# x_b of two chunks by DMA instead of by selection, and another order of the opening

## The reference

```python
Ws = [W0, W1, W2]                       # W0 40x40x100, W1 and W2 40x100x100
curr = base = inputs                    # 512 x 40 x 16
for Wk, bk in zip(Ws, bs):
    z = jnp.einsum('bid,bjd->bdij', base, curr)
    curr = jnp.einsum('bdij,ijh->bhd', z, Wk) + bk[None, :, None]
    logit.append(curr)
pooled = jnp.sum(jnp.concatenate(logit, axis=1), axis=-1)
out = pooled @ lin_w + lin_b            # 512 x 1
```

## Time and profile before

| | us |
|---|---|
| median of 3 runs | 181.58 |
| lowest and highest run | 181.56, 182.77 |
| profiled execution | 181.67 |
| its span | 179.9 |

### The profile page before, as it was taken

How to read it: one execution, slowest core, us unless ns; L and a number is a source line. 1 busy time by engine, 2 the same in 40 slices (tenths; PEclk the granted TensorE clock), 3 DMA queues, 4 the chain that set the end, 5 groups by cost and what they waited for, 6 DMA issues and landing times.

```text
span 179.9 us, 2520 instructions
## 1 busy us (share of the span) xinstructions
PE 175.2 (97%) x798; PEld 118.7 (66%) x798; DVE 152.1 (85%) x138; ACT 73.7 (41%) x79; POOL 13.0 (7%) x20
## 2 busy tenths in 40 slices
PE   6999989999999999999999999999999999999994
PEld 2374557777777777777777777677777777777760
DVE  0696896399999999999999999999999999993022
ACT  2535750064642464236432644264426442530021
POOL 3631624000000000000000000000000000000000
PEclk9999999999999999999999999999999999999999
DMA  5998834999978587857795778477957740000000
GB/s 188 381 413 317 231 87 120 417 416 410 281 229 296 163 236 227 319 141 230 229 327 143 233 226 315 149 231 225 283 182 233 226 133 0 0 4 0 0 0 0
DMA packets 12038, 37.06 MB, mean 206 GB/s; under 512 B 2481, under 2 KB 3325, under 8 KB 12030
## 3 DMA queue, kind: packets, MB, share of 16 engines
q1 hardware_dynamic: 11066, 36.36, 61.4%
q10 hardware_dynamic: 868, 0.32, 0.8%
q0 software_dynamic: 96, 0.27, 0.6%
HBM read 35.88 MB, written 1.07 MB: 205 GB/s over the span
## 4 chain that ended last, share of the span: by engine, by line
PE 95%; POOL 1%; issue 1%; DVE 1%; ACT 1%; ACTq 0%; DVEq 0%; POOLq 0%
PE c_ps L456 42%; PE q_ps L456 42%; PE q_ps L509 4%; PE q_ps L544 2%; PE c_ps L500 1%; PE q_ps L500 1%; POOL wc_low L422 1%; PE q_ps L520 1%; PE q_ps L465 1%; PE q_ps L547 1%; PE c_ps L594 1%; PE c_ps L597 0%; DVE acc L326 0%; DVE w_post L270 0%; ACT out_sb L404 0%
## 5 line engine op out<-in xcount | busy, mean ns | idle before, releaser
L337 ACT ACTIVATE z_high<-xb_z 126x1024 fp32r<-126x1024 f32 x56 | 59.2, 1061 | 79.3 <-DVE xb_z L249 79.1
L256 DVE TENSOR_TENSOR z_low<-xb_z,z_high 126x1024 fp32r<-126x1024 f32 x56 | 68.9, 1233 | 0.9 <-ACT z_high L337 0.8
L249 DVE TENSOR_TENSOR xb_z<-x_a,xb_z 126x1024 f32<-126x1024 f32 x50 | 61.0, 1220 | 9.4 <-DMA xb_z<-xw 9.3
L456 PE MATMUL c_ps<-z_high,wc_high 126*101 126x512 f32 x112 | 35.4, 396 | 0.7 <-POOL wc_low L422 0.7
L456 PE MATMUL c_ps<-z_low,wc_high 126*101 126x512 f32 x112 | 35.0, 394 | 0.0
L456 PE MATMUL c_ps<-z_high,wc_low 126*101 126x512 f32 x112 | 35.0, 394 | 0.0
L456 PE MATMUL q_ps<-z_high,wq_high 126*101 126x512 f32 x108 | 33.9, 395 | 0.0
L456 PE MATMUL q_ps<-z_high,wq_low 126*101 126x512 f32 x108 | 33.8, 394 | 0.0
L456 PE MATMUL q_ps<-z_low,wq_high 126*101 126x512 f32 x108 | 33.7, 393 | 0.0
L456 PEld LDWEIGHTS c_ps<-z_high,wc_high 126*101 126x101 f32 x112 | 18.3, 165 | 9.1 <-POOL wc_low L422 1.2
L456 PEld LDWEIGHTS c_ps<-z_high,wc_low 126*101 126x101 f32 x112 | 18.5, 165 | 7.5
(11 more groups left out here) (56 smaller groups left out, 60.6 us busy)
## 6 DMA issues: line engine op xcount, KB each, us to landing
xb_z<-xw SPq DMA_DIRECT2D x50, 512.0 KB, 4.3
x_a<-xa SPq DMA_DIRECT2D x8, 512.0 KB, 4.9
w_post<-w1x SPq DMA_DIRECT2D x4, 512.0 KB, 8.6
w_d<-w2h SPq DMA_DIRECT2D x4, 404.0 KB, 6.1
pair_sb<-w_pairs SPq DMA_DIRECT2D x1, 404.0 KB, 11.6
d_dram<-w_d SPq DMA_DIRECT2D x2, 189.4 KB, 2.8
d_dram<-w_d SPq DMA_DIRECT2D x4, 94.7 KB, 2.6
pair_sb<-d_dram ACTq DMA_DIRECT2D x3, 82.9 KB
```

The source lines that it names most:

```text
L249: nc.vector.tensor_tensor(xb_z[0:K, c, :], x_a[0:K, u % 2, :], x_b, ALU.mult).then_inc(z_done, 1)
L256: nc.vector.tensor_tensor(z_low[0:K, m % SLOTS, :], xb_z[0:K, c, :], z_high[0:K, m % SLOTS, :].bitcast(fp32), ALU.subtract).then_inc(low_d ...
L337: nc.scalar.activation(z_high[0:K, m % SLOTS, :], xb_z[0:K, m % C, :], ACT.Copy).then_inc(high_done, 1)
L456: last = nc.tensor.matmul(ps[0:J, h * B:(h + 1) * B], w[0:K, c * J:(c + 1) * J], z[0:K, slot, h * B:(h + 1) * B], start=(c == 0 and k == 0 ...
```

## The change

- x_b of chunks 5 and 6 of unit 0 is loaded by SP behind W0's last piece; TensorE makes the selections 1 to 4 only. Form 5 and form 6 wait for these loads.
- Warm-up: 12 matmuls instead of 20, then one fp32 matmul on acc. V piece 0 goes ahead of selections 1 and 2.
- SP: the four loads of W2 go ahead of W0's second piece. One 25 KB store of D goes from POOL to SP.
- VectorE: split 2 goes ahead of form 3, split 3 ahead of form 5, and the copy of d group 2 is done by VectorE behind form 4, with a semaphore of its own.
- ScalarE: select_r is rounded before chunk 0, round_high(0, 2) goes ahead of the copy of the v rows, cast_w0(1) behind the copies of v and the constant, round_high(0, 3) ahead of copy_d(3).
- POOL: low_w0(0) goes ahead of sum_w0(1).

```diff
--- before.py
+++ after.py
@@ -18,6 +18,7 @@
 BODY = 2 * C
 PRODUCT_AT = 16
 C1_AT = 2 * C - 1
+SELECTED = 4
 
 VP = 4
 VG = 5
@@ -41,7 +42,7 @@
 RIGHT = P + T - 1 + C - 1 - F
 DW = LEFT + F + RIGHT
 DB = 48
-DS_SP, DS_POOL = 7, 3
+DS_SP, DS_POOL = 8, 2
 WC_CUTS = (0, 1, 3, C)
 WQ_CUTS = (0, 2, C)
 PREP_CUTS = (0, 2, 4, C)
@@ -51,7 +52,7 @@
 
 LOW_AT = 64
 SW = 128 + C - 1
-WARM = 20
+WARM = 12
 E_AT = 0
 Z_AT = E_AT + DR
 ZW = QT + VG
@@ -135,6 +136,7 @@
         const_done = sem("const_done")
         const_copied, select_rounded = sem("const_copied"), sem("select_rounded")
         dgroup_done, dgroup_copied = sem("dgroup_done"), sem("dgroup_copied")
+        dgroup_copied_dve = sem("dgroup_copied_dve")
         wc_sums, wc_highs, wc_ready = sem("wc_sums"), sem("wc_highs"), sem("wc_ready")
         wq_sums, wq_highs, wq_ready = sem("wq_sums"), sem("wq_highs"), sem("wq_ready")
         last_sums, last_highs, last_ready = sem("last_sums"), sem("last_highs"), sem("last_ready")
@@ -193,21 +195,24 @@
             load_xb(0, 0)
             load_w0(0)
             sp.dma_start(small_sb[:, :], small).then_inc(small_loaded, 16)
-            load_w0(1)
             for i in range(VP):
                 load_w2(i)
+            load_w0(1)
             for i in W1_ORDER:
                 load_w1(i)
             load_w0(2)
+            for c in range(SELECTED + 1, C):
+                load_xb(0, c)
             sp.wait_ge(dgroup_copied, 1)
             store_d(sp, 0, LEFT + 4 * GI, 4 * GI, LOWER - 4 * GI, (8, 8 + DB))
             sp.wait_ge(dgroup_copied, 3)
             store_d(sp, 0, LEFT, 0, 2 * GI, (0, DB))
             store_d(sp, 1, LEFT + UPPER_AT[0], 0, 2 * GI, (DR - DB, DR))
-            sp.wait_ge(dgroup_copied, 4)
+            sp.wait_ge(dgroup_copied_dve, 1)
             store_d(sp, 0, LEFT + 2 * GI, 2 * GI, GI, (0, DB))
             store_d(sp, 1, LEFT + UPPER_AT[2], 2 * GI, GI, (DR - DB, DR))
-            sp.wait_ge(dgroup_copied, 5)
+            store_d(sp, 1, 0, 3 * GI - (LEFT - 2 * GI), LEFT - 2 * GI, (0, 32))
+            sp.wait_ge(dgroup_copied, 4)
             store_d(sp, 0, LEFT + 3 * GI, 3 * GI, GI, (4, 4 + DB))
             store_d(sp, 1, LEFT + UPPER_AT[3], 3 * GI, GI, (10, 10 + DB))
             sp.wait_ge(equals_cleared, 1)
@@ -240,11 +245,11 @@
 
                 u, c = divmod(m, C)
                 dve.wait_ge(xa_loaded[u % 2], it * 16 + 16 * (u // 2 + 1))
-                if 0 < m < C:
+                if 0 < m <= SELECTED:
                     dve.wait_ge(selected, m)
                     x_b = sel_ps[m % 2][0:K, :]
                 else:
-                    dve.wait_ge(xb_loaded[c], it * 32 + 16 * (u if c > 0 else u + 1))
+                    dve.wait_ge(xb_loaded[c], it * 32 + 16 * (u + 1 if c == 0 or c > SELECTED else u))
                     x_b = xb_z[0:K, c, :]
                 nc.vector.tensor_tensor(xb_z[0:K, c, :], x_a[0:K, u % 2, :], x_b, ALU.mult).then_inc(z_done, 1)
 
@@ -274,6 +279,11 @@
                 dve.wait_ge(xa_high, 1)
                 nc.vector.tensor_tensor(x_split[LOW_AT:K], x_a[LOW_AT:K, 0, :], x_split[LOW_AT:K].bitcast(fp32),
                                         ALU.subtract).then_inc(xa_split, 1)
+
+            def copy_d(g):
+                dve.wait_ge(dgroup_done, D_ORDER.index(g) + 1)
+                nc.vector.tensor_copy(w2_d[:, g * GI * J:(g + 1) * GI * J], d_ps[D_ORDER.index(g) % 2]
+                                      ).then_inc(dgroup_copied_dve, 1)
 
             def first_weights(i):
 
@@ -302,12 +312,14 @@
             form(0, 1)
             form(0, 2)
             split(0, 1)
+            split(0, 2)
             form(0, 3)
             form(0, 4)
+            copy_d(2)
+            split(0, 3)
             form(0, 5)
-            split(0, 2)
             form(0, 6)
-            for m in range(3, C):
+            for m in range(4, C):
                 split(0, m)
             first_weights(0)
             first_weights(1)
@@ -358,12 +370,12 @@
 
             act.wait_ge(xa_loaded[0], 16)
             nc.scalar.activation(x_split[0:K], x_a[0:K, 0, :], ACT.Copy).then_inc(xa_high, 1)
-            round_high(0, 0)
             act.wait_ge(small_loaded, 16)
             nc.scalar.activation(select_r[:, :], select_sb, ACT.Copy).then_inc(select_rounded, 1)
+            round_high(0, 0)
             cast_w0(0)
-            cast_w0(1)
             round_high(0, 1)
+            round_high(0, 2)
             act.wait_ge(v_multiplied, 1)
             nc.scalar.activation(v_rows[:, :], v_ps, ACT.Copy).then_inc(v_rows_copied, 1)
             act.wait_ge(const_done, 1)
@@ -371,13 +383,12 @@
             nc.scalar.activation(v_sb[:, :], vt_ps, ACT.Copy).then_inc(v_copied, 1)
             nc.scalar.activation(const_sb[:, :], const_ps, ACT.Identity, bias=linb,
                                  scale=float(D)).then_inc(const_copied, 1)
+            cast_w0(1)
             copy_d(4)
             copy_d(0)
             copy_d(1)
-            round_high(0, 2)
-            copy_d(2)
+            round_high(0, 3)
             copy_d(3)
-            round_high(0, 3)
             cast_w0(2)
             for m in range(4, BODY):
                 if m == GATHER_AT:
@@ -423,15 +434,13 @@
                                         chunks(wc_high, c0, c1).bitcast(fp32), ALU.subtract).then_inc(wc_ready, 1)
 
             sum_w0(0)
+            low_w0(0)
             sum_w0(1)
-            low_w0(0)
             low_w0(1)
             pool.wait_ge(dgroup_copied, 3)
             store_d(pool, 0, LEFT + F, 0, RIGHT, (32, DR), d_stored_pool)
             store_d(pool, 1, LEFT - 2 * GI, 0, 2 * GI, (0, 32), d_stored_pool)
             sum_w0(2)
-            pool.wait_ge(dgroup_copied, 4)
-            store_d(pool, 1, 0, 3 * GI - (LEFT - 2 * GI), LEFT - 2 * GI, (0, 32), d_stored_pool)
             low_w0(2)
             pool.wait_ge(wc_ready, len(WC_CUTS) - 1)
             nc.gpsimd.memset(q_sides[0:P, 1, 0:J], 0.0).then_inc(equals_cleared, 1)
@@ -511,6 +520,7 @@
             def v_piece(i):
 
                 if i == 0:
+                    pe.wait_ge(small_loaded, 16)
                     nc.tensor.matmul(v_ps[0:QT, :], lw2_hot, lw2_row, start=True, stop=False)
                 pe.wait_ge(w2_loaded[i], 16)
                 for n in range(2 * i, 2 * i + 2):
@@ -551,9 +561,11 @@
             pe.wait_ge(filled, 1)
             for _ in range(WARM):
                 warm()
+            pe.wait_ge(acc_done, 1)
+            nc.tensor.matmul(warm_ps[0:J, :], acc[:, 0:J], acc[:, 0:B], start=True, stop=True)
+            v_piece(0)
             select_xb(1)
             select_xb(2)
-            v_piece(0)
             v_piece(1)
             c1_chunk(0, 0)
             v_piece(2)
@@ -565,9 +577,7 @@
             d_group(4)
             d_group(0)
             d_group(1)
-            select_xb(5)
             d_group(2)
-            select_xb(6)
             d_group(3)
             for m in range(1, C):
                 c1_chunk(0, m)
```

## The result

Median of 20 runs 181.94 us, against 181.57 for the kernel before: ratio 1.0031, interval 1.0021 to 1.0040. (The ratios here are worked out from all runs and are not quotients of two medians; that quotient is 1.0020.) The profiled execution took 182.42 us (span 180.6), 0.48 above its median; the kernel before stays within 0.1 of its own. The runs of the changed kernel spread more, 181.43 to 183.27.

A forecast was written before the change was run, and what follows sets the result against it. TensorE was taken as the bound (95% of the chain), so only the start of q chunk 0 mattered. All terms were 0 except the D stores' +0.27: 181.67 + 0.27 = 181.94, rounded to 181.9 us, range 180.6 to 183.2.

The forecast's parts named there:

- a gap before c1 chunk 4: Sign listed as wrong: TensorE idle before c1 chunk 4, marking the rival that forms 5 and 6 hold VectorE's queue.
- d group 3 before 18.0: Sign listed as wrong: TensorE's d group 3 starting before 18.0 us; expected at 18.2, when W1's last piece lands.
- Opening of TensorE: TensorE's work before q chunk 0: c1 chunk 3 starts 0.95 us earlier, at 22.65, so q chunk 0 could start at 28.3.
- the two landings that I took as fixed: DMA landings before c1: W1's last piece at 18.2 us and W0's last piece at 19.15 us.
- V rows: Warm-up and first work: half a microsecond gained ahead of the v rows, given away by ScalarE's earlier rounding; 0 in all.
- VectorE, 0 to 0.1: VectorE's reordered list with forms 5 and 6 waiting for x_b loads: splits 4 to 6 just fit, costing 0 to 0.1 us.
- The rival that form 6 holds VectorE's list: Late x_b of chunk 6 delays VectorE's split 4 and q chunk 0: 181.9, or 183.3 if later still; chance 0.06.
- Stores of D, gathers at 24.5: SP's queue: stores behind the x_b loads hold the gathers until 24.5 us, q chunk 0 at 29.5, +0.27 us.
- the packed estimate: DMA queue ideally packed: 17.1 + 2.54 of loads + 3.85 of stores + 0.7 to land, last store at 24.2 us.
- The queue absorbs the loads: Rival at SP's D stores: they land by 22.9 us, TensorE's 28.3 counts, 180.7 us in all; chance 0.22.
- Unit 1, slack 0.5, no stall: Start of unit 1: loads 0.7 us later, TensorE 0.27 later, slack falls from 0.93 to 0.5, no stall.
- No change beyond 1%: Whole kernel: time within about 1% (1.8 us) of the kernel before, counted as the same; chance 0.90.

The follow-up runs named there:

- e3: Changed kernel with selections 5 and 6 made by TensorE again and both x_b loads still queued but unused, small store on SP: 181.91 us, ratio 1.0026.
- e11: Changed kernel with all six selections on TensorE, both x_b loads queued but unused, and the 25 KB store back on POOL: 182.13 us, ratio 1.0029.
- e8: Changed kernel with 8 warm matmuls filling TensorE's gap ahead of c1 chunk 3: 182.00 us, ratio 1.0023.
- e5: Changed kernel without the x_b loads, all six selections on TensorE, and the 25 KB store back on POOL: 180.47 us, ratio 0.9936.
- e1: Changed kernel without the x_b loads, all six selections on TensorE, 25 KB store kept on SP: 181.20 us, ratio 0.9974.
- e6: Changed kernel with only chunk 6's x_b loaded, chunk 5 by TensorE's selection, 25 KB store on SP: 181.17 us, ratio 0.9972.
- e9: Changed kernel with both x_b loads kept and the 25 KB store back on POOL: 181.91 us, ratio 1.0015.
- e2: Kernel before with only the two x_b loads added and selections 5 and 6 removed, all orders as before: 185.34 us, ratio 1.0217.
- e4: Changed kernel with the two x_b loads issued by ScalarE's queue instead of SP's: 184.49 us, ratio 1.0172.
- e7: Kernel before with the two x_b loads, without selections 5 and 6, plus 12 warm matmuls in TensorE's gap before c1 chunk 2: 184.06 us, ratio 1.0133.
- e10: Changed kernel with only chunk 6's x_b loaded and the 25 KB store back on POOL: 181.01 us, ratio 0.9967.
- e12: Kernel before with only the 25 KB store moved from POOL to SP: 181.62 us, ratio 1.0007.

## Why the prediction was right, and where it was not

The time is 181.94 for 181.9, and the wait that the sum turns on, the gathers behind the last store of D, is the one that e3 and e11 show. But that the number came out to 0.04 us is partly luck: two parts of the store term were off in ways that cancelled, and two signs that the prediction itself had listed under "wrong" did show in the profile, a gap before c1 chunk 4 and d group 3 before 18.0. e8's profile has the forecast's times almost to the letter: d group 3 at 18.18 (18.2), gathers at 24.54 (24.5), q chunk 0 at 29.38 (29.5); only its c1 chunk 3 is later, for the filler.

- **Opening of TensorE (own work 0.93 earlier).** Confirmed where nothing else stands in the way: e5 starts q chunk 0 at 28.26. But it is the new orders that do it, W0's low part being done sooner; the two selections fewer bring nothing on this path, since c1 chunk 3 starts at 22.55 and 22.70 in e3 and e5 with all six, and with no gap before it. In the changed kernel's profile the two landings that I took as fixed moved: W1's last piece came at 7.3 + 9.8 = 17.1 and not 18.2, W0's at 19.8 and not 19.15. They move from run to run: in e8, with the same loads, they came at 18.13 and 19.16. One trace had given both numbers. The five W1 loads of the changed kernel, first and last issue, and shortest, median and longest time to landing:

```profile
L192 SPq DMA_DIRECT2D w_post<-w1x x5: 441/459/652, 5.1 to 7.3; - x5
...
DMA to landing us min/median/max: 6.9/8.2/9.8
```

 So the gap before c1 chunk 3 grew to 1.94 and chunk 3 started at 23.09, not 22.65.
- **V rows, 0.** They were copied at 13.03, 0.25 earlier; it counted for nothing, since wc_low held c1 chunk 3.
- **VectorE, 0 to 0.1.** This term failed: about 0.7 stands where it had 0 to 0.1, hidden behind the gathers. Form 5 began at 20.99 (20.4 expected), form 6 took 1.86 us instead of 1.22, beside POOL's low part, and c1 chunk 4 waited 0.70 for split 4. The rival that form 6 holds VectorE's list was half true: with it TensorE ends c1 at about 29.63, 0.13 before wq_low. The prediction had TensorE idle for 1.2 us in front of q chunk 0; the gaps stood ahead of chunks 3 and 4 instead. e3 and e11 show that without this wait the time is no shorter.
- **Stores of D, gathers at 24.5.** Measured 25.01 in the changed kernel's profile and 24.54 in e8's, and the wait is the one named. But its parts were mis-sized. The 3.85 us of full DMA time were too many: with work queued the engines moved loads and stores at 382 GB/s, and nearly all of them were done by 22.6 (share 0.14 from there to 22.7), where the packed estimate had 23.5. Why the same stores had taken a share of 0.97 at only 223 GB/s from 18 to 19 us in the kernel before is not shown; thin issues alone do not explain it. The engine that trails cost about 1.6 us on top, where I took 0.3 of a possible 1.3. "The queue absorbs the loads" was right for nearly all engines, and the prediction's last two stores at "2.8 and 2.1 us" are a misreading (2.1 and 2.4, and 2.8 is POOL's), without effect, since both end at 23.3. The Trainium skill (DMA: Bandwidth & Descriptors, Anatomy of one DMA) gives the sum of that rival for DMAs that POOL issues, and seven of the ten stores in the kernel before were SP's; what the prediction set against it, 279 GB/s of full use, was no limit.
- **Unit 1, slack 0.5, no stall.** There is 0.11 left (39.54 against 39.65), for the loads of unit 1 began at 30.84, 1.5 us later than before, and not 0.7.
- **No change beyond 1%:** right, the ratio is 1.0031.

What stays open: why SP's store issues sometimes take 1.0 to 1.75 us. It was seen in e1, e6, e8, e9, e11 and the changed kernel, with seven and with eight stores on SP and with and without the loads, and in none of the profiles of the kernel before, e2, e3, e4, e5, e7, e10 and e12 (0.87 at most). The spread of the runs does not follow it: 0.5 us in e6, which has an issue of 1.53, and 2.7 in e3, which has none. Which engine trails, and why, the profile does not show either. That e5 gains 0.73 over e1 is measured; that the long issues are the whole of it is not shown, nor why the store's place matters with no load (0.73) and hardly with one or two (0.16 and 0.03).

## What to carry to other kernels

Before putting loads into a hole of a DMA queue, ask who waits for the last landing of what is behind them: a wait for all of ten stores waits for the slowest of 16 engines, and here a fuller queue made that one 1.6 us later while the others were done as early as before. Undo the parts of a bundled change one by one: here the orders, with the small store left where it was, gained 1.1 us and the loads gave 1.4 back. And where TensorE must stand still for 2 to 3 us, the bill can be the gap and the slow matmuls behind it; in e7 warm matmuls in the gap took 1.3 us of it away.

## What the runs showed of the hardware

**Clock.** In e2 the granted clock fell from 1.00 to 0.50 (2.4 to 1.2 GHz) at 23.7, late in a standstill of 2.95 us, and stayed there for about 3.4 us, although matmuls ran again from 24.07. Gaps of 1.87 and 0.69 were followed by the same in one run of e9, and 1.94 and 0.70 were not in the changed kernel's profile.

**VectorE beside POOL.** Form 6 with x_b from SBUF, beside POOL's low part of W0, took 1.86 us, and the low part 1.62. In e5 the same form takes its x_b from PSUM, and the two rows, VectorE's and POOL's, are

```profile
20.85 1.22 DVE L253 TENSOR_TENSOR xb_z<-x_a,q_ps 126x1024 f32<-126x1024 f32 x1
```

```profile
21.41 0.98 POOL L432 TENSOR_TENSOR wc_low<-pair_sb,wc_high 126x404 fp32r<-126x404 f32 x1 [0.21 <-ACT wc_high L367]
```

1.22 and 0.98. The low part is 0.98 to 0.99 in all four profiles where form 6 takes x_b from PSUM (e1, e3, e5, e11), and 1.62 to 1.78 in the changed kernel, e8 and e9, where it takes it from SBUF. The Trainium skill (GPSIMD Engine Reference, Specifications) says that POOL shares its SBUF interfaces with VectorE and contends with VectorE's instructions that have two SBUF inputs; the traces agree. So a load instead of a selection also moved an operand from PSUM to SBUF, which against e5 is 0.6 us more on each of the two engines, at the place where both were wanted. In the kernel before, splits 3 and 4 met the low part in the same way: it took 1.56 us, and split 4 took 1.76.
